# A feature map formed as max(y + 1, exp(min(y, 0))) in one VectorE operation out of PSUM

## The reference

```python
def _feature_map(x):
    return jax.nn.elu(x) + 1.0
q = _feature_map((x @ Wq.T + bq)...)      # b, head, t, 32
k = _feature_map((x @ Wk.T + bk)...)
v = (x @ Wv.T + bv)...
kv_cum = cumsum(einsum('bhtd,bhte->bhtde', k, v), axis=2)
numerator = einsum('bhtd,bhtde->bhte', q, kv_cum)
denominator = einsum('bhtd,bhtd->bht', q, cumsum(k, axis=2))
out = numerator / maximum(denominator, EPS)
return out @ Wo.T + bo
...
x = x + layernorm(attention(layernorm(x)))
x = x + layernorm(ffn(layernorm(x)))      # ffn: x and weight rounded per block of 32
```

## Time and profile before

| what | value |
|---|---|
| median of 3 runs (lowest to highest) | 2689.52 us (2688.79 to 2692.34) |
| profiled execution: its own time | 2689.53 us |
| its span, first to last instruction | 2687.7 us |
| mean granted TensorE clock | 0.991 of full speed |
| DMA, mean over the span | 40 GB/s |

### The profile page before, as it was taken

How to read it: one execution, slowest core, us unless ns; L and a number is a source line. 1 busy time by engine, 2 the same in 40 slices (tenths; PEclk the granted TensorE clock), 3 DMA queues, 4 the chain that set the end, 5 groups by cost and what they waited for, 6 DMA issues and landing times.

```text
span 2687.7 us, 62620 instructions
## 1 busy us (share of the span) xinstructions
PE 2503.3 (93%) x24082; PEld 2061.4 (77%) x24082; DVE 2171.5 (81%) x4175; ACT 1255.2 (47%) x2314; POOL 1092.2 (41%) x1482
## 2 busy tenths in 40 slices
PE   5999999999999999999999999999999999999996
PEld 4777778777778777778777787777777777877775
DVE  6778888788888788888888887888888888878885
ACT  4444445444454444454444544444544445444442
POOL 1343444334443334443344433444434444333443
PEclk8999999999999999999999999999999999999998
DMA  4011100111011111001111011110111110111000
GB/s 148 21 40 47 41 29 31 39 47 43 30 36 39 39 47 43 27 31 39 47 47 32 30 39 39 47 43 27 36 38 44 47 34 28 39 39 47 31 25 24
DMA packets 57483, 107.55 MB, mean 40 GB/s; under 512 B 6768, under 2 KB 7152, under 8 KB 56816
## 3 DMA queue, kind: packets, MB, share of 16 engines
q1 hardware_dynamic: 57456, 107.18, 12.3%
HBM read 73.60 MB, written 33.55 MB: 40 GB/s over the span
## 4 chain that ended last, share of the span: by engine, by line
PE 43%; DVE 29%; issue 11%; POOL 9%; ACT 6%; DVEq 1%; POOLq 0%; DMA 0%; ACTq 0%; SPq 0%
PE work L343 9%; PE work L345 8%; PE work L344 8%; DVE kc L829 6%; PE score L434 4%; DVE KT L812 4%; PE work L460 4%; PE work L360 4%; PE work L453 3%; DVE A L872 3%; POOL xd L1061 2%; DVE bn_r L789 2%; DVE amax L897 2%; POOL rs_r L1042 2%; DVE QT L812 2%
## 5 line engine op out<-in xcount | busy, mean ns | idle before, releaser
L872 DVE TENSOR_TENSOR A<-score,causal 128x512 f32<-128x512 f32 x512 | 317.5, 683 | 42.3 <-PE score L434 42.2
L597 ACT ACTIVATE o_buf<-x_res,shift_r,rs_r 128x512 f32<-128x512 f32 x128 | 104.7, 818 | 409.2 <-POOL shift_r L1045 409.2
L1052 POOL TENSOR_TENSOR x_res<-x_res,o_buf 128x512 f32<-128x512 f32 x128 | 179.3, 1401 | 210.4 <-ACT o_buf L597 210.4
L593 ACT CAST xT_hi<-work 128x512 fp32r<-128x512 f32 x128 | 74.8, 584 | 384.5 <-PE work L360 384.5
L343 PE MATMUL work<-wv_hi,xT_hi 128*128 128x512 f32 x512 | 216.1, 422 | 0.0
L343 PE MATMUL score<-xT_hi,wk_hi 128*128 128x512 f32 x512 | 206.6, 403 | 6.2 <-issue 6.2
L1042 POOL TENSOR_TENSOR rs_f<-ve_f,minus_half 128x1 f32<-128x1 f32 x128 | 70.3, 549 | 343.9 <-DVE ve_f L793 343.9
L1042 POOL TENSOR_TENSOR rs_r<-ve_r,minus_half 128x1 f32<-128x1 f32 x128 | 96.3, 753 | 278.5 <-DVE ve_r L793 278.5
L343 PE MATMUL score<-xT_hi,wq_hi 128*128 128x512 f32 x512 | 206.5, 403 | 0.0
L343 PE MATMUL work<-wo_hi,oT_hi 128*128 128x512 f32 x512 | 202.7, 396 | 2.9 <-DVE oT_lo L879 2.6
L344 PE MATMUL work<-wv_lo,xT_hi 128*128 128x512 f32 x512 | 202.0, 394 | 0.0
(11 more groups left out here) (130 smaller groups left out, 6957.9 us busy)
## 6 DMA issues: line engine op xcount, KB each, us to landing
x_in<-in_x SPq DMA_DIRECT2D x128, 256.0 KB, 2.8
x_res<-in_x SPq DMA_DIRECT2D x128, 256.0 KB, 2.6
out<-f_buf SPq DMA_DIRECT2D x96, 256.0 KB, 2.0
out<-xd SPq DMA_DIRECT2D x32, 256.0 KB, 2.0
V<-in_wk SPq DMA_DIRECT2D x1, 1024.0 KB, 7.8
QT<-in_wq SPq DMA_DIRECT2D x1, 1024.0 KB, 8.7
kc<-in_wo SPq DMA_DIRECT2D x1, 1024.0 KB, 10.2
A<-in_wf SPq DMA_DIRECT2D x1, 1024.0 KB, 11.9
```

What stands on the lines that cost most here:

```text
L872: nc.vector.tensor_tensor(A[:, j, :, :], score_bank[j][:], causal[:].unsqueeze(1).to_broadcast([P, G, P]), ALU.mult).then_inc(a_set, 1)
L1052: nc.gpsimd.tensor_tensor(x_res[:, b, :], x_res[:, b, :], o_buf[:, b % 2, :], ALU.add).then_inc(r_set, 1)
```

## The change

The feature map is formed as max(y + 1, exp(min(y, 0))). ScalarE keeps two passes, `exp_t = relu(-y)` and `exp_t = exp(-exp_t)`; the pass `dst = relu(y)` is gone. VectorE's operation reads `exp_t` and the projection itself from PSUM, adds bias + 1 (a value per partition, prepared in the prologue) and takes the maximum: one `scalar_tensor_tensor` in place of one `tensor_tensor`. Since VectorE is now the last reader of the k projection's bank, TensorE's `q(g)` waits for `k_set`, which `phi_k(g)` raises.

```diff
+        bias_q_plus_1 = sb("bias_q_plus_1", [P, G])
+        bias_k_plus_1 = sb("bias_k_plus_1", [P, G])
...
                 def q(g):
                     if cur:
-                        pe.wait_ge(k_act, count(i, g))
+                        pe.wait_ge(k_set, count(i, g))
                         weights(i, "q")
                         by_feature("q", g).then_inc(q_mm, 1)
...
-                def feature_map(m, g, dst, mm, added, clamped, exp_done, done):
+                def clamped_exp(m, g, mm, added, clamped, exp_done):
...
                     nc.scalar.activation(exp_t[:, g % 2, :], y, ACT.Relu, bias=minus_bias[:, g:g + 1],
                                          scale=-1.0).then_inc(clamped, 1)
-                    nc.scalar.activation(dst, by_seq(y), ACT.Relu, bias=bias[:, g:g + 1]).then_inc(done, 1)
                     act.wait_ge(clamped, count(i, g))
                     nc.scalar.activation(exp_t[:, g % 2, :], exp_t[:, g % 2, :], ACT.Exp,
                                          scale=-1.0).then_inc(exp_done, 1)
...
-                def phi(dst, g, done, added):
-
-                    dve.wait_ge(done, count(i, g))
-                    nc.vector.tensor_tensor(dst, by_seq(exp_t[:, g % 2, :]), dst, ALU.add).then_inc(added, 1)
+                def phi(dst, g, bias_plus_1, exp_done, done):
+
+                    dve.wait_ge(exp_done, count(i, g))
+                    nc.vector.scalar_tensor_tensor(dst, by_seq(score_bank[g][:].rearrange("p g t -> p (g t)")),
+                                                   bias_plus_1[:, g:g + 1], by_seq(exp_t[:, g % 2, :]),
+                                                   ALU.add, ALU.max).then_inc(done, 1)
...
+            nc.vector.tensor_scalar(bias_q_plus_1[:], bias_q[:], 1.0, None, ALU.add)
+            nc.vector.tensor_scalar(bias_k_plus_1[:], bias_k[:], 1.0, None, ALU.add)
```

More of the change, by code:

```diff
@@ L184, in build @@
         q_exp = sem("q_exp")
-        k_act = sem("k_act")
-        q_act = sem("q_act")
         kn_set = sem("kn_set")
@@ L608, in turn @@
                 first = isinstance(i, int) and i == 0
-                def feature_map(m, g, dst, mm, added, clamped, exp_done, done):
-                    bias, minus_bias = {"q": (bias_q, minus_bias_q), "k": (bias_k, minus_bias_k)}[m]
+                def clamped_exp(m, g, mm, added, clamped, exp_done):
+                    minus_bias = {"q": minus_bias_q, "k": minus_bias_k}[m]
                     act.wait_ge(mm, count(i, g))
@@ L631, in k @@
                             added = (q_set, count(i - 1, g + 2))
-                        feature_map("k", g, tokens(KT, g), k_mm, added, k_clamped, k_exp, k_act)
+                        clamped_exp("k", g, k_mm, added, k_clamped, k_exp)
                 def q(g):
@@ L636, in q @@
                         added = (q_set, count(i, g - 2)) if g >= 2 else (k_set, count(i, g + 2))
-                        feature_map("q", g, by_seq(QT[:, g, :]), q_mm, added, q_clamped, q_exp, q_act)
+                        clamped_exp("q", g, q_mm, added, q_clamped, q_exp)
                 def kn(b):
@@ L807, in turn @@
                 first = isinstance(i, int) and i == 0
-                def phi(dst, g, done, added):
-                    dve.wait_ge(done, count(i, g))
-                    nc.vector.tensor_tensor(dst, by_seq(exp_t[:, g % 2, :]), dst, ALU.add).then_inc(added, 1)
+                def phi(dst, g, bias_plus_1, exp_done, done):
[3 more added lines that the diff above has]
+                                                   ALU.add, ALU.max).then_inc(done, 1)
                 def phi_k(g):
                     if cur:
-                        phi(tokens(KT, g), g, k_exp, k_set)
+                        phi(tokens(KT, g), g, bias_k_plus_1, k_exp, k_set)
                 def phi_q(g):
                     if cur:
-                        phi(by_seq(QT[:, g, :]), g, q_exp, q_set)
+                        phi(by_seq(QT[:, g, :]), g, bias_q_plus_1, q_exp, q_set)
                 def scan(g):
```

## The result

The changed kernel takes 2630.54 us (median of 4 runs, 2629.54 to 2634.45) against 2689.91 us (4 runs): a ratio of 0.9782, 95% interval 0.9770 to 0.9793. The forecast was 2631.5 us, so the total was right to 1 us. That closeness is in part luck: two effects that the prediction lacked, one of each sign, and a step that it made too short nearly cancel, as the experiments show.

A forecast was written before the change was run, and what follows sets the result against it. TensorE, busy 93%, is nearly full, so only its idle time can be won: denominators 1.87 us earlier in each of 31 turns, 58.0 us, giving 2689.5 - 58.0 = 2631.5 us; range 2615 to 2676.

The forecast's parts named there:

- The operation's price: VectorE's feature-map scalar_tensor_tensor on 128x512 takes 0.75 us, 0.06 above an undisturbed addition.
- The collision: With one tensor input in SBUF, VectorE's phi_k(3) no longer waits for GpSimd and falls from 1.78 to 0.75 us.
- The exponential: On ScalarE it starts 0.71 us behind its first pass instead of 1.15, the second Relu gone: 0.44 us earlier.
- Step 2: VectorE's xdT_lo ends 1.29 us earlier, so TensorE's first gap, 1.14 us before f(1), closes.
- Steps 3 to 5: VectorE, not ScalarE's exponential, sets the start of phi_q(3); TensorE's denominators start 1.87 us earlier, some 1.3 us idle stay.
- Nothing is lost behind the denominators: Behind the denominators TensorE paces the others, so the whole turn keeps the 1.87 us and the third gap stays.
- The lock stays: Rival, 12%: the scalar or opcode makes VectorE's operation wait for GpSimd, phi_k(3) 1.85 us long; gain 16 us, 2674.
- The moved collision: Rival, 14%: VectorE's product(2) or product(3) runs into GpSimd's f_buf + x_res, paying 1.1 us; gain 24 us, 2666.
- The slow operation: Rival, 8%: each nanosecond above 0.69 us counts eight times a turn on VectorE; at 1.21 us an operation, 2745.
- Given back: Rival, 6%: another wait, for instance xT_lo and the norms before k(0), takes the 1.87 us a turn; 2689.

The follow-up runs named there:

- the padded kernel: The kernel before with two unused 128x4 tiles where the change has its new ones, filled in the prologue: 2696.91 us (1.0030).
- the pass dropped: The kernel before without the second Relu pass; VectorE adds exp_t to exp_t, both in SBUF, leaving out the relu(y) term: 2686.22 us (0.9993).
- two halves: The changed kernel with its new tiles last and each feature-map operation cut into two of 128x256: 2655.86 us (0.9876).
- the kernel with `scan(3)` ahead: The changed kernel with its new tiles last and, on VectorE, scan(3) ahead of phi_q(0): 2591.60 us (0.9637).

## Why the prediction was right

- *The operation's price, 0.75 us*: right, median 0.751 and 0.743. The Trainium skill's rule that a PSUM source costs 62 cycles more (VectorE: DVE Perf Modes, on the TRN2 errata) would have had 0.81. The measured 0.751 disagrees with it for this operation too.
- *The collision*: right. `phi_k(3)` went from 1.78 to 0.74, never above 0.753. The kernel that keeps the pass has this effect by itself, and against the kernel before with like addresses it saves 47.8 us (2696.91 - 2649.16), more than the 34 I had worked out for it. TensorE's two waits fell by just these 34 (60.0 to 46.8 and 28.6 to 7.5 us). Some 5 of the other 13 us are three stretches at the lower clock (below) that only the padded kernel has; the rest was not followed.
- *The exponential, 0.44 us earlier*: right in place and size (0.70 instead of 1.15 behind the first pass). What it is worth I had treated as a term of its own. It is not: alone it gives nothing that can be measured (2686.22 against 2688.27), on top of the free operation it gives 18.6 us (2649.16 - 2630.54), and the difference goes with the collisions of `phi_k(1)` and `phi_q(3)` that it runs into.
- *Step 2, the gap before `f(1)`*: right, closed in every turn. `xdT_lo` ends at 22.51 us behind `k(0)`'s start, 1.37 earlier than before (1.29 forecast).
- *Steps 3 to 5, the denominators*: the right engine, VectorE, sets the start, and they come 2.06 us earlier (1.87 forecast). Of the missing 0.2, 0.05 is there at `phi_k(1)` already (11.40 us behind `k(0)`'s start instead of 11.83, 0.43 where 0.38 was forecast), and 0.1 comes from `phi_q(3)`, which no longer waits and so starts 0.07 us behind the start of `ve_x` (1261.45, 1261.52), ahead of its end. With the addresses kept, the wait left is 1.3 us a turn as forecast.
- *Nothing is lost behind the denominators*: wrong, the one step that failed. From there to the next `k(0)` the slower spacing of TensorE's matmuls takes 0.39 us. Of it the prediction had nothing, since the two tiles in the prologue were costed only as two operations, "not in the loop and count as nothing". What they cost is their tiles' place, 13.6 us.
- *Why the sum came out all the same*: (2543.3 - 59.9) / 31 = 80.11 us a turn after, (2602.3 - 61.6) / 31 = 81.96 before, 1.85 less, by the first and last starts of the denominators' matmuls (below). But an ordinary turn is 1.67 less. The other 0.18 is the granted clock. In four turns of the loop of the profiled kernel before it fell to half, its lower level of 1.2 GHz, for 3.4 us, and such a turn takes 83.3 us.

The denominators' matmuls of both kernels, first and last start at the end of the row; then the granted clock (PEclk, the third number from the end of the row) of one such stretch of the kernel before and of the like place in another turn:

```profile
L409 PE MATMUL work<-kc,den_sel x1024: 269/273/423, 61.6 to 2602.3; 128*32 128x128 f32 x171
```
```profile
L409 PE MATMUL work<-kc,den_sel x1024: 269/273/421, 59.9 to 2543.3; 128*32 128x128 f32 x171
```
```profile
227.00:230.30 3.30, 3.30 (x36) 2.64 (x37) 2.29 (x5) 0.00 (x0) 0.00 (x0) 0.50 0.36 109
1292.50:1295.80 3.30, 3.26 (x42) 2.70 (x43) 3.11 (x7) 0.00 (x0) 0.06 (x1) 1.00 0.31 119
```

The stretch at 227 begins with the denominators' matmuls at 226.96, behind TensorE's 2.12 us of idle time. Most turns have this idle time without a stretch behind it. In the changed kernel it is 0.89 us, the clock is 1.00 at the like place (1263.10 to 1266.40), and no turn inside the loop has such a stretch. The other profiles go the same way: with 2.12 us of idle time before the denominators (the pass dropped) seven turns have one, with 1.99 (the padded kernel before) three, with 1.83 (two halves) one, and with 1.55 or less none in eight kernels. That the shorter idle time is the cause fits this and was not tested by itself. So 1.67 x 31 = 52 us are shorter turns and some 6 us (4 x 1.6) a clock that no longer falls. Neither the 13.6 us lost to the addresses nor these 6 us were in the sum, and the steps to the denominators were short by 0.2 x 31 = 6; that loss and these two gains nearly cancel by luck. With the addresses kept, the same change is worth 71 us (2616.92 against 2688.27), which is 58 + 6 + 6 and 1 more.
- *The lock stays, 12%*: it did not happen. Its price of 16 us had the flaw of my step for the kernel with the pass dropped: with the lock in place the earlier exponential gave 2 us at most.
- *The moved collision, 14%*: it did not happen in the changed kernel, where product(3) takes 0.69 us. An operation that starts earlier and so runs into GpSimd is what ate the gain of the kernel with the pass dropped.
- *The slow operation, 8%*: did not happen, but its slope was about right (38.9 us measured for 0.13 us more, 32 by it).
- *Given back, 6%*: the wait for `xT_lo` did stay where it was (28.4 us). What was given back, 0.39 us a turn, was TensorE's own slower spacing, which this rival did not name.

## What to carry to other kernels

- In these runs no elementwise VectorE operation with one input straight from PSUM was held up by GpSimd (256 of them, none above 0.753 us), while the addition with both inputs in SBUF was, by 1.1 us once a turn. Where the trace has a VectorE operation at two and a half times its median, look for what GpSimd does at that time and whether one of the operation's inputs could come from PSUM.
- Before a pass is taken away so that something starts sooner, look up what the other engine does at the new time: the same edit was worth nothing where the operation behind it could be held up, and 19 us where it could not.
- In this kernel two new small tiles were better allocated last, by 13.6 us; it costs nothing to try. Compare the spacing of matmuls in a block between two profiles before a difference is explained by the order of the work.

## What the runs showed of the hardware that was not expected

- Matmuls of 128x512 in the blocks of `o(b)` started 227 ns apart or 233, depending on where in SBUF their operand lay: shifts by 32, 64 and 128 bytes a partition all gave the slower spacing, with the granted clock at its upper level. In the blocks of `k` and `q` the shift by 32 bytes gave 229, those by 64 and 128 gave 232 to 234.
- In the profile of the kernel before, the granted clock fell to its lower level for 3.4 us in four turns of 31, each time within 0.2 us of the start of the denominators' matmuls; it cost 1.6 us each.
- GpSimd and a scan on VectorE hold each other up too: product(0) takes 2.09 us beside `scan(3)` and at most 1.31 in the kernel with `scan(3)` ahead, and the 4-element copy behind the scan waits for that product, 1.07 us instead of 0.17.
- A ScalarE pass that waits for the pass right in front of it starts 0.03 us behind its end (1260.62 to 1260.65). The forecast was 0.04, with the possibility left open that nothing would be gained.
